# Attention over batch elements: the first layer's finish moved behind the exponent's input, row factors made two tiles ahead

## What is computed

```
x  = x + s * g                       # end of layer one
xn = (x - mean(x)) / sqrt(var(x) + eps)
# attention of layer two: "sequence" is the first axis, of length 4
q, k, v = xn @ Wq.T + bq, xn @ Wk.T + bk, xn @ Wv.T + bv     # 16 heads of 16
scores  = einsum('ibhd,jbhd->ijbh', q, k) / sqrt(16)          # causal over i, j in 0..3
ex      = exp(scores - max_j(scores))
attn    = ex / (1 + sum_j(ex))
out     = einsum('ijbh,jbhd->ibhd', attn, v)
logits  = xn @ wg                                             # router of the expert layer
```

## Time and profile before

| | us |
|---|---|
| median of 3 runs | 1510.79 (1509.65 to 1512.31) |
| the profiled execution | 1510.5 |
| its span in the trace | 1508.7 |
| first attention sum (L956, t = 0) begins | 366.02 |
| the sum of t = 13 begins | 600.87 |

### The profile page before, as it was taken

One profiled execution on the slowest core, in us unless ns is written; L12 is line 12 of the kernel. 1 busy time (PEld: TensorE's weight loads), 2 busy tenths in 40 slices (PEclk: granted clock), 3 DMA queues, 4 the chain that ended last, 5 costly groups with the idle time before them and its releaser, 6 DMA issues. The chain is left out here.

```text
span 1508.7 us, 23107 instructions
## 1 busy us (share of the span) xinstructions
PE 1219.6 (81%) x7479; PEld 811.8 (54%) x7479; DVE 1007.7 (67%) x1829; ACT 619.5 (41%) x933; POOL 684.8 (45%) x577
## 2 busy tenths in 40 slices
PE   2999997758888888433899999999899999999800
PEld 1655664436666666312466666666566665666500
DVE  2777774035888888787567756667666765676547
ACT  0555553223444444100545544554544454464321
POOL 2122220003777777701345554454555544555559
PEclk9999998659999999755899999999999999999955
DMA  9000002300000001010655555464455545556577
GB/s 309 1 0 0 0 0 114 165 15 29 29 29 29 29 29 30 15 56 22 144 82 96 106 106 98 70 133 82 89 107 106 109 65 130 85 90 106 77 199 258
DMA packets 156359, 122.20 MB, mean 81 GB/s; under 512 B 88400, under 2 KB 147664, under 8 KB 154864
## 3 DMA queue, kind: packets, MB, share of 16 engines
q1 hardware_dynamic: 116128, 77.61, 17.5%
q0 software_dynamic: 25200, 35.85, 16.6%
q10 hardware_dynamic: 14944, 7.62, 1.8%
HBM read 58.91 MB, written 44.30 MB: 68 GB/s over the span
## 5 line engine op out<-in xcount | busy, mean ns | idle before, releaser
L1652 ACT ACTIVATE e_h_all<-e_pH,e_b1c,e_h_scale 128x512 f32<-128x512 f32 x256 | 199.7, 780 | 279.3 <-PE e_pH L1693 277.2
L1707 PE MATMUL e_pY<-e_w_hi,e_h_hi 128*128 128x256 f16 x1024 | 281.2, 275 | 12.8 <-DVE e_w_lo L1527 12.6
L1451 POOL DMA_INDIRECT expert_sums<-e_yo,e_dcol x128 | 210.5, 1644 | 168.1 <-DVE e_yo L1605 132.8
L1709 PE MATMUL e_pY<-e_w_hi,e_h_lo 128*128 128x256 f16 x1024 | 280.7, 274 | 0.0
L1708 PE MATMUL e_pY<-e_w_lo,e_h_hi 128*128 128x256 f16 x1024 | 280.6, 274 | 0.0
L1437 POOL DMA_INDIRECT e_xg<-xn_rows,e_icol x140 | 161.8, 1156 | 195.9 <-DVE e_icol L1468 163.1
L1570 DVE TENSOR_TENSOR e_h_lo<-e_h_all,e_h_hi 128x512 f16<-128x512 f32 x256 | 176.9, 691 | 61.6 <-ACT e_h_hi L1652 48.9
L1691 PE MATMUL e_pH<-e_xT,e_w_hi 128*128 128x512 f16 x512 | 195.8, 382 | 22.1 <-DMA e_xT<-e_xs 15.4
L1692 PE MATMUL e_pH<-e_xT,e_w_hi 128*128 128x512 f16 x512 | 195.8, 382 | 0.0
L1693 PE MATMUL e_pH<-e_xT,e_w_lo 128*128 128x512 f16 x512 | 195.5, 382 | 0.0
L1707 PEld LDWEIGHTS e_pY<-e_w_hi,e_h_hi 128*128 128x128 f16 x1024 | 100.7, 98 | 37.6 <-DVE e_h_lo L1570 19.7
(11 more groups left out here) (231 smaller groups left out, 2235.9 us busy)
## 6 DMA issues: line engine op xcount, KB each, us to landing
raw<-expert_w SPq DMA_DIRECT2D x18, 1024.0 KB, 6.2
expert_sums<-r_zero SPq DMA_DIRECT2D x10, 1024.0 KB, 12.7
xn_rows<-c_xn SPq DMA_DIRECT2D x16, 512.0 KB, 3.0
f_ya<-expert_sums SPq DMA_DIRECT2D x16, 512.0 KB, 5.6
out<-f_ya SPq DMA_DIRECT2D x16, 512.0 KB, 3.9
x_st<-x ACTq DMA_DIRECT2D x4, 1536.0 KB, 13.9
e_xg<-xn_rows,e_icol POOLq DMA_INDIRECT x140
e_xT<-e_xs SPq DMA_TRANSPOSE x136
```

What stands on the lines that cost most here:

```text
L1451: pool.indirect_dma_start(v.y_dram, bass.IndirectOffsetOnAxis(dcol[u][:, q:q + 1], axis=0), yo[:, q, :], None, bounds_check=N + CAP - 1, o ...
L1652: last = act.activation(dst, pH[h % NPH][:, :], ACT.Relu, bias=b1c[eu][:, h:h + 1], scale=h_scale[eu][:, 0:1])
L1707: pe.matmul(pY[:, q, :], h_hi[:, h, cols], w2_hi[:, h, :], start=(h == 0), stop=False)
L1709: last = pe.matmul(pY[:, q, :], h_lo[:, h, cols], w2_hi[:, h, :], start=False, stop=(h == HT - 1))
```

## The change

On VectorE, `layer0(t + 2)` moves from the head of tile t to the place behind the subtraction that makes the exponent's input, ahead of the sum over the exponents. On GpSimd, `scale` is called for t + 2 at the head of the tile, ahead of the product with v, in place of t + 3 in the middle of it, and the prologue makes two tiles' factors in place of three. No instruction's shape changes; the total of each is the same.

```diff
@@ GpSimd @@
-                for t in range(3):
-                    scale(t, t % 2, reused=t >= 2)
+                for t in range(2):
+                    scale(t, t % 2, reused=False)

                 def body(i, u, left):
                     t = 2 * i + u

                     n = 0
+                    if left >= 2:
+                        scale(t + 2, u)
                     pool.wait_ge(att_ready, t + 1)
                     for j in range(B):
                         ...
-                        if j == 1 and left >= 3:
-                            scale(t + 3, 1 - u)
@@ VectorE @@
                 def body(i, u, left):
                     t = 2 * i + u
-                    if left >= 2:
-                        layer0(t + 2)
                     dve.wait_ge(k_evac, t + 1)
                     dve.wait_ge(q_evac, t + 1)
                     ...
                                       ALU.subtract).then_inc(ex_in, 1)
+                    if left >= 2:
+                        layer0(t + 2)
                     dve.wait_ge(ex_out, t + 1)
```

## The result

The changed kernel takes 1582.3 us (median of 4 runs, 1581.78 to 1582.79), the kernel before 1510.22 us in the same rounds: a ratio of 1.0476, interval 1.0458 to 1.0494. Slower by 72 us, as forecast (1582). The profiled execution took 1581.78 us, its span is 1580.0 us.

The account below looks back on a forecast made before the run. Bound by a ring of TensorE and ScalarE through k, 18.07 us a step; the change makes a longer ring through VectorE. 1510.5 us plus 52.3 (longer steps) plus 19.5 (TensorE's clock) gives 1582.3 us, range 1560 to 1600.

Parts of the forecast that it names:

- Layer0 behind the subtraction: VectorE's exponent wait: k must wait for L892, so subtraction to sum takes 7.38 us, or 8.80 with a table load.
- the old ring: TensorE's and ScalarE's loop from one taking of k to the next, 16.93 us; steps of 18.07 us before the change.
- The products directly behind att: VectorE's q and k products start with GpSimd's product with v: 7.67 us; products' start to subtraction's end 12.08 us.
- The step: Per tile of the attention loop: 12.08, 7.38 and 2.08 us make 21.54 us; last sum 52.3 us later, table loads included.
- The clock: TensorE idles about 4.6 us ahead of each k and runs it slower: 1.5 us a step, 19.5 us over 13.
- Row factors at no cost: GpSimd's scale() at the tile's head, 1.95 us: delays neither the product with v nor the normalising; cost nothing.
- three terms: In the attention loop: k held through L892, VectorE's products meeting GpSimd's, and TensorE's slower clock; together 52.3 plus 19.5 us.
- VectorE's ring: New loop through products, subtraction, L892, k and sum: 21.54 us a step, longer than 16.93 us, so it sets the pace.
- Rival A: VectorE's q and k products: no contention, they stay near 4.2 us; step 18.16 us, 1519 us in all; chance 0.08.
- rival D: Attention loop: no change, TensorE's and ScalarE's ring keeps the pace, 1511 us; chance 0.04.
- Rival C: VectorE's exponent wait: it is filled and the kernel gets faster, step 15.98 us, 1483 us; chance 0.04.

Follow-up runs that it names:

- split: Changed kernel with layer0 cut in two, L892 back at the tile's head, addition and statistics behind the subtraction: 1518.96 us, ratio 1.0056 to the kernel before.
- pool_held: Changed kernel with GpSimd's product with v held until the next tile's products of q and k are done: 1506.92 us, ratio 0.9977 to the kernel before.
- warm8: Changed kernel with 8 idle products on TensorE between q and the wait ahead of k: 1571.5 us, ratio 1.0416 to the kernel before.
- pool_only: Kernel before with only GpSimd's half of the change, VectorE's order as before: 1516.27 us, ratio 1.0032.
- layer0_only: Kernel before with only VectorE's half of the change, GpSimd's order as before: 1578.72 us, ratio 1.0443.
- held_logits: pool_held with ScalarE's logits copy and recurrence states moved ahead of taking q and k: 1493.36 us, ratio 0.9886 to the kernel before.
- held_split_logits: held_logits with layer0 cut in two, L892 at the tile's head and the rest behind the subtraction: 1518.08 us, ratio 1.0041 to the kernel before.
- logits: Kernel before with ScalarE's logits copy and recurrence states moved ahead of taking q and k: 1487.14 us, ratio 0.9840.

## Why the prediction was right

*Layer0 behind the subtraction.* Right. k's start hangs on L892 in all 13 steps, the wait for the exponent became longer and not shorter. That this is needed for the loss is shown by `split`. The claim that VectorE touches the old ring at one point only was too strong: ScalarE's taking of q also waits for VectorE's products (in 7 tiles of the kernel before), but k came later than that, so it cost nothing here.

*The products directly behind att.* Right, 7.69 us for 7.67 us forecast. That it is needed too is shown by `pool_held`. The lock of the Trainium skill ("SBUF — State Buffer", section "SBUF: two separate sides") would have given 8.22 us; the trace of after agrees with the row of before, half a microsecond under it.

*The step.* Forecast 21.54 us, 0.55 us for the table load and 1.5 us for the clock, 23.59 us; measured 23.62 us. The last sum was forecast near 672 and came at 673.25. The mechanism is right; that the mean fits to 0.03 us is luck, since errors of both signs cancel: steps without a table load were forecast at 23.04 us and took 22.87, those with one at 24.46 us and took up to 25.3, and the last took 21.88.

*The clock.* Forecast 1.5 us a step, between bounds of 0 and 2.1; `warm8` gives 1.41 us as a net figure, k's own length 1.68 us. The idle time ahead of k's weight load was 4.3 us on average (55.8 us in 13 tiles) and 4.6 us at most; 4.6 was worked out.

*Row factors at no cost.* Right only in its small claim. No engine waited for them in the changed kernel. But `pool_only` costs 5 us by another way, the longer products, and `layer0_only` ran 3.6 us faster than both halves together. My working asked who waits for the moved instructions, and not whom they had kept apart where they stood. This step was incomplete; its size lay inside the range of the forecast.

*How the terms add up.* The forecast summed three terms, and the sum was right. The experiments show that they are not a sum in general:

| kernel | L892 behind the subtraction | products meet GpSimd's | us over before |
|---|---|---|---|
| before | no | little | 0 |
| split | no | yes | 8 |
| pool_held | yes | no | -4 |
| the change | yes | yes | 72 |

Each alone is nearly swallowed by the old ring of 18.07 us. Together they make VectorE's ring the longer one, 21.54 us as reckoned, and the clock's 1.4 to 1.7 us follow from the idle time that this makes. Rival A, the change without the meeting, was forecast at 1519 us and ran at 1506.92: it reckoned 4.2 us for the products where, with GpSimd held, they take 3.0 us. The same slip stands in rival D, which gives 18.2 us for VectorE's ring "even without any contention": the 4.21 us were measured beside GpSimd's small instructions. With 3.0 us it is the 16.9 us of the expectation of `pool_held`, the old ring keeps the pace, and that is what `pool_held` showed. Rival C, that the filled wait is won, is answered by `split`: the wait was filled and nothing was won.

## What to carry to other kernels

Before work is put into an engine's wait, find what ends that wait and follow it back: if it passes through the moved work itself, the wait moves with it. And read off what the moved piece had kept apart: here one instruction group separated two engines that slow each other, and two effects that cost at most 8 us alone became 72 us together. A wait off the ring that sets the pace gives nothing when it is filled; shorten the ring first (here 24 us by taking two copies, and the table load with them, out of it), and then look at the waits again.

## What the runs showed that I had not expected

- Holding GpSimd back by 3.2 us, so that it does not meet VectorE, cost nothing in time: its product took less time alone (first instruction 1.93 us for 2.89 us). That was so only where its later work was not awaited.
- Letting L892, with one input in PSUM, run first beside GpSimd's first product did not shorten the meeting: the products still took 7.2 to 7.7 us in `split`.
- Row factors cost nothing in the changed kernel. In `held_logits` and `held_split_logits`, where GpSimd is held back and the factors stand behind its late product, ScalarE waited for them, up to 3.6 us in the one and up to 6.2 us in the other.
- A table load of 1.28 us in ScalarE's loop stood in the ring in every other tile and cost TensorE a slow stretch on top; in `logits`, where it follows the taking of k and VectorE sets the pace, it left no trace in the steps (16.47 us with and without it).
